# Moving the first batch of cross-attention into the last unit of self-attention, and turning the product of scores and exponentials

## The chip, the cores and the metric

The kernel runs on one core of a Trainium2 chip. The metric is the device time of one execution in microseconds. The core has TensorE (PE, matrix products into PSUM), VectorE (DVE), ScalarE (ACT), GpSimd (POOL) and SyncE (SP, which here only issues DMAs). Each engine runs its own list of instructions in order; they wait for each other through semaphores that the code sets by hand.

## The reference

One decoder layer over x of shape (8, 256, 512) in float32, three residual steps:

```
x = x + self_attention(layernorm(x))     # 16 heads of 128; slots M = 64, causal, rope
x = x + cross_attention(layernorm(x), ctx, mask)   # 16 heads of 16, 512 x 512 scores per head and batch
x = x + feed_forward(layernorm(x))       # weights through an NF4 round trip, silu gate
```

Self-attention, per head, with q and k turned by rope and es = exp(clip(s)), enz = 1 / cumsum(es):

```
A  = causal(q @ k.T) * scale             # t x j
ok = enz * (A @ es)                      # t x 64
qv = softmax(ok)
W2 = causal((qv * enz) @ es.T)           # t x j
o  = W2 @ v;  y = (rmsnorm(o) * silu(g)) @ Wo.T     # q, k, v, g, s are projections of layernorm(x)
```

Cross-attention projects q from layernorm(x), k and v from ctx, with a mask on both sides, and takes a softmax over 512 positions.

## The kernel before, in words

`decoder` calls `self_attention`, `cross_attention` and `feed_forward`, each a block of its own; between two blocks all engines meet, and POOL clears the semaphores of the old block.

**Self-attention** works in 32 units n: two halves of the tokens, eight groups g of two heads, two token blocks p of 512. Each engine has a function `unit(n, g, p, k0)` written by hand, which also holds the second stage of unit m = n - 1 and the third of unit l = n - 2, so that the engines' chains overlap. `units` calls it for the first three units and the last of each half, and in a hardware loop for those between; `core(LAST, 1)` then drains what is left of unit 31. Projections are done in split precision: a value's high part (fp32r) is made by ACT, its low part by POOL, and three products of four matrix steps replace one. On PE a unit is: `project_qk` 0, `project_s` (scores of ws2), `project_out` tiles 0 and 1 of unit l, `ok(m)`, `project_qk` 1, `project_out` 2 and 3, transposes of es, `project_qk` 2, transposes of qv, and so on to `out_transposes(m)` (the letters in `a_ogh`, `a_ogl` are the high and low parts of unit l's gated output, made by ACT and POOL out of these transposes).

`ok(m)` (L969 to L971) multiplies for each head and pair of token blocks: stationary a block of 128 x 128 of `a_aw` (masked scores), moving 64 columns of `a_es`. The result lies in PSUM (`pok`, the fourth bank of `a_mid`) with tokens on the partitions. DVE scales it by enz (`okn`, L676) and takes the maximum (L680), POOL subtracts it (L552), ACT takes exp (L447), POOL multiplies by enz (L558), PE transposes it (L996). DVE's units of the loops carry 31 instructions each of the NF4 round trip of the feed-forward weights besides, in fixed places (`nf4`).

In four units (`PREPS`) the next 512 tokens are normalised, transposed and split into `xh` and `xl`; the tile `xs` holds the raw tokens.

**Cross-attention** starts with the rows of the mask (`mask_products`, L1478 to L1493, 8 partitions x 512), stored to DRAM (`rows_scratch`). For each batch: layernorm, six products (`project(b, j)`: j = 0, 1 for q, 2, 3 for k, 4, 5 for v, plain float32), split of q and k into `hi` (ACT) and `lo` (POOL), stored to DRAM (`parts_scratch`, `put_part`) and loaded again as stacks `Q[b % 3]` and `K[b % 3]`, in which 48 rows of a head's three-part product and 5 or 6 rows of the mask stand below each other (`fill_stack`, `mask_rows`). Then 32 quarters t (four heads each): `row_scores` on PE and `row_max` on DVE find each row's maximum two quarters ahead (LEAD = 2), `turn_max` transposes them, DVE negates them (`max_rows`), SP stores and loads them as the last row of Q (`rows`), and only then `dot` and the exponential may run. All loads and stores but a few stand in one list on SP, in the order in which the code issues them.

The head of cross-attention before is: project(0, 0 to 5), wait for stack 0, scores of unit 0, `turn_max(0)`, project(1, 0 to 5), scores of unit 1, dots.

## Time and profile before

| | us |
|---|---|
| median of 3 runs | 2444.95 |
| lowest, highest | 2437.4, 2446.93 |
| the profiled execution | 2442.58 |
| its span | 2440.8 |
| PE busy | 2211.7 (91%) |
| DVE busy | 1612.8 (66%) |
| ACT, POOL busy | 776.0 (32%), 756.5 (31%) |

Self-attention fills the time up to about 1468 us, cross-attention runs from 1478 to about 2120, feed-forward to the end. Busy times are sums over stages with different limits, so a row of the whole span only says where to look; the stretch in question is read from the instructions in order of time. There each row has its start, its duration, the engine, the line of the kernel, output and inputs, the shapes and a count; the bracket at the end is the idle time of the engine in front of the row and what ended it. Products overlap by their ends, so the distance between two starts says more than a duration.

### The profile page before, as it was taken

Reading aid. Unit: us, or ns where it says so; the run is one execution under the profiler, and the core shown is the slowest. Engines: PE = TensorE matmul, PEld = TensorE weight load, DVE = VectorE, ACT = ScalarE, POOL = GpSimd, SP = SyncE. Lnnn points to the kernel's source line nnn. Section 1 sums busy time; section 2 is a strip of 40 time slices with the busy share of each in tenths; the row PEclk is TensorE's granted clock in tenths of the full one; section 3 lists DMA queues with packets and bytes.
Section 4 is the critical chain, followed back from the end, with each engine's and each line's share of the span. In section 5 each row is a group of like instructions: output and inputs, shape, how many; then the busy total and the mean of one; then the engine's idle time right before and its main releaser. Section 6 shows DMA issues by size and latency. Waiting matters only on the chain. (4 is left out here: it accounts for less than half of the span.)

```text
span 2440.8 us, 35529 instructions
## 1 busy us (share of the span) xinstructions
PE 2211.7 (91%) x11766; PEld 1577.0 (65%) x11766; DVE 1612.8 (66%) x2879; ACT 776.0 (32%) x1804; POOL 756.5 (31%) x531
## 2 busy tenths in 40 slices
PE   6899999999999999999999973788988897679998
PEld 4778888888877888888888861333333332257777
DVE  6668788888866568878887733567777777442221
ACT  1213323222332332232223120154454555532221
POOL 3324433433442443453353322111112221111222
PEclk9899999999999999999999986688788998869999
DMA  5211101101111201110110006825565554301100
GB/s 186 84 38 50 49 13 55 50 15 47 49 50 62 70 15 42 49 55 6 55 49 18 3 18 150 137 82 102 117 127 124 120 107 90 101 35 52 52 35 18
DMA packets 58085, 157.21 MB, mean 64 GB/s; under 512 B 9510, under 2 KB 24302, under 8 KB 51446
## 3 DMA queue, kind: packets, MB, share of 16 engines
q1 hardware_dynamic: 56742, 153.55, 23.7%
q10 hardware_dynamic: 1248, 2.46, 0.6%
q8 instruction: 52, 0.85, 0.2%
q14 instruction: 43, 0.35, 0.1%
HBM read 113.25 MB, written 34.33 MB: 60 GB/s over the span
## 5 line engine op out<-in xcount | busy, mean ns | idle before, releaser
L1501 DVE TENSOR_REDUCE x_mx<-x_pm 128x1 f32<-128x512 f32 x512 | 316.1, 679 | 76.5 <-PE x_pm L1598 75.3
L1334 ACT ACTIVATE x_E<-x_pd 128x512 f32<-128x512 f32 x512 | 265.5, 603 | 226.6 <-PE x_pd L1612 225.6
L1598 PE MATMUL x_pm<-x_K,x_Q 53*128 53x512 f32 x512 | 191.2, 514 | 44.7 <-DMA x_K<-parts_scratch 24.7
L659 DVE TENSOR_TENSOR a_rm<-a_pj,a_rope 128x1024 f32<-128x1024 f32 x128 | 155.8, 1218 | 113.0 <-PE a_pj L930 111.4
L1612 PE MATMUL x_pd<-x_Q,x_K 54*128 54x512 f32 x512 | 180.5, 514 | 49.8 <-DMA x_Q<-maxima_scratch 25.0
L1612 PEld LDWEIGHTS x_pd<-x_Q,x_K 54*128 54x128 f32 x512 | 76.9, 203 | 225.3 <-ACT x_E L1334 116.2
L442 ACT ACTIVATE a_v<-a_pj 128x256 f32<-128x256 f32 x128 | 49.1, 384 | 414.6 <-PE a_pj L946 414.6
L568 POOL TENSOR_TENSOR a_ogl<-a_ogf,a_ogh 128x512 fp32r<-128x512 f32 x64 | 81.3, 1291 | 292.7 <-ACT a_ogf L473 292.7
L1626 PE MATMUL x_pa<-x_E,x_vx 128*32 128x512 f32 x1024 | 153.4, 675 | 0.0
L930 PE MATMUL a_pj<-a_xh,a_wqk_h 128*128 128x512 f32 x512 | 150.8, 416 | 1.3 <-POOL a_wqk_l L538 1.3
L946 PE MATMUL a_pj<-a_wvg_h,a_xh 128*128 128x512 f32 x512 | 151.0, 417 | 1.0 <-DVE a_rm L659 1.0
L930 PE MATMUL a_pj<-a_xh,a_wqk_l 128*128 128x512 f32 x512 | 140.9, 397 | 0.0
L946 PE MATMUL a_pj<-a_wvg_l,a_xh 128*128 128x512 f32 x512 | 140.5, 396 | 0.0
L930 PE MATMUL a_pj<-a_xl,a_wqk_h 128*128 128x512 f32 x512 | 140.3, 396 | 0.0
L946 PE MATMUL a_pj<-a_wvg_h,a_xl 128*128 128x512 f32 x512 | 140.1, 395 | 0.0
L1598 PEld LDWEIGHTS x_pm<-x_K,x_Q 53*128 53x128 f32 x512 | 81.8, 210 | 89.4 <-DVE x_mx L1501 56.1
L720 DVE TENSOR_TENSOR a_acc<-a_po,a_acc 128x512 f32<-128x512 f32 x128 | 88.2, 689 | 66.2 <-PE a_po L1049 66.0
L1732 POOL TENSOR_TENSOR f_hl<-f_hf,f_hh 128x512 fp32r<-128x512 f32 x44 | 56.6, 1285 | 212.2 <-ACT f_hh L1773 212.2
L1049 PE MATMUL a_po<-a_wo_h,a_ogh 128*128 128x512 f32 x256 | 106.5, 416 | 16.2 <-POOL a_ogl L568 16.2
L665 DVE RECIPROCAL a_enz<-a_mid 128x512 f32<-128x512 f32 x32 | 107.2, 3351 | 7.8 <-PE a_mid L914 7.8
L1373 POOL TENSOR_TENSOR x_lo<-x_lo,x_hi 128x512 fp32r<-128x512 f32 x32 | 40.7, 1271 | 231.1 <-ACT x_hi L1329 231.1
L930 PEld LDWEIGHTS a_pj<-a_xl,a_wqk_h 128*128 128x128 f32 x512 | 96.5, 189 | 23.7
(209 smaller groups left out, 4919.4 us busy)
## 6 DMA issues: line engine op xcount, KB each, us to landing
a_qk_raw<-in_wqk SPq DMA_DIRECT2D x16, 1024.0 KB, 5.4
a_vg_raw<-in_wvg SPq DMA_DIRECT2D x16, 1024.0 KB, 4.9
x_Q<-parts_scratch SPq DMA_DIRECT2D x42, 256.0 KB
x_K<-parts_scratch SPq DMA_DIRECT2D x42, 256.0 KB
a_wo_raw<-in_wo SPq DMA_DIRECT2D x16, 512.0 KB, 3.6
parts_scratch<-x_hi SPq DMA_DIRECT2D x16, 512.0 KB, 2.8
parts_scratch<-x_lo SPq DMA_DIRECT2D x16, 512.0 KB, 3.3
a_acc<-in_w SPq DMA_DIRECT2D x6, 704.0 KB, 4.5
```

What stands on the lines that cost most here:

```text
L568: nc.gpsimd.tensor_tensor(ogl[:, h, :], ogf[:, h, :], ogh[:, h, :].bitcast(F32), ALU.subtract).then_inc(ogl_done, 1)
L659: nc.vector.tensor_tensor(turned, pb, table, ALU.mult).then_inc(roped_m, 1)
L665: nc.vector.reciprocal(enz[:, p], ps[:, 0, :].rearrange("p (t m) -> p t m", t=4)).then_inc(enz_done, 1)
L720: nc.vector.tensor_tensor(a, po[:, tt % 2, :], a, ALU.add).then_inc(added, 1)
L930: last = mm(pj[:, j % 2, :], wa[:, c, j * P:(j + 1) * P], xa[:, c, p * UT:(p + 1) * UT], start=k == 0, stop=k == 11)
L946: last = mm(pj[:, tt % 2, :], xa[:, c, t0:t0 + P], wa[:, c, :], start=k == 0, stop=k == 11)
L1049: last = mm(po[:, tt % 2, :], oa[:, h, tt * P:(tt + 1) * P], wa[:, h, :], start=k == 0, stop=k == 5)
L1334: nc.scalar.activation(E[:, n % ESLOTS, :], pd[:, n % 3, :], ACT.Exp, scale=XD ** -0.5).then_inc(exp_done, 1)
L1501: nc.vector.reduce_max(mx[:, u % 2, at:at + 1], pm[:, k % 3, :], AX_X).then_inc(pm_done, 1)
L1598: mm(pm[:, k % 3, :], Q[b % 3][z, hp, q * P:(q + 1) * P], K[b % 3][z, hp, :], start=True, stop=True).then_inc(pm_ready, 1)
L1612: mm(pd[:, n % 3, :], K[b % 3][z, hp, q * P:(q + 1) * P], Q[b % 3][z, hp, :], start=True, stop=True).then_inc(dot_ready, 1)
L1626: last = mm(pa[32 * i:32 * i + 32, 0, :], vx[:, b % 3, q, head(t, i)].rearrange("p d k -> p (d k)"), E[:, k % ESLOTS, :], start=q == 0, st ...
```

## The change

1. `ok(m)` is turned: stationary 64 columns of `a_es`, moving the 256 or 128 columns of `a_aw`. Head 0 writes PSUM partitions 0 to 63, head 1 partitions 64 to 127. The result has the slots on the partitions, so ACT copies it to a new tile `okT` (`turned_ok`) and PE transposes it back (`transposes_ok`) into the same bank. It stands in front of the output products of unit l, the transposes behind them.
2. Except in the units of `PREPS`, `project_s` on PE and `clip` on DVE are first in their unit.
3. The mask rows are made at the start of the kernel by DVE, in lines of tiles that are not yet in use, and stored to DRAM in eleven stores; no row is computed in cross-attention.
4. In the last unit DVE and POOL normalise the first batch of cross-attention (`variances(4)`, `normalised(4)`), which SP has loaded into `xs` with the first batch of ctx. In `core` PE does its four products of q and k (`project_cross`), DVE evacuates them (`take_cross`), ACT and POOL split them, SP stores the parts and fills stack 0.
5. `xh` and `xl` of self-attention and the stacks Q0 and K0 are views of one tile `q_big` that lives over all three parts (in feed-forward it holds w3 and xh). SP waits at the end of self-attention until the stack is filled.
6. Cross-attention starts with the scores of unit 0; then come the two products of v of batch 0, `turn_max(0)`, project(1, 0 to 5), scores of unit 1. Stack 1 is filled in six steps during the first six quarter steps, behind the maxima. Statistics and normalisation of later batches are split over two steps each.

What is the order in a unit of self-attention on PE? Before (L1036 transposes of the gated output, L930 the first product of q, L903 the scores, L1049 the output products of which 12 stand here, L969 ff. ok):

```order
L1036 MATMUL a_po<-a_ident,a_gs 128x128 x8
L930 MATMUL a_pj<-a_xh,a_wqk_h 128x512 x4
L930 MATMUL a_pj<-a_xh,a_wqk_l 128x512 x4
L930 MATMUL a_pj<-a_xl,a_wqk_h 128x512 x4
L903 MATMUL a_mid<-a_ws2x,a_s1x 128x128 x4
L1049 MATMUL a_po<-a_wo_h,a_ogh 128x512
...
L969 MATMUL a_mid<-a_es,a_aw 128x64
L970 MATMUL a_mid<-a_es,a_aw 128x64
```

After, the same place (L1057 was L903, L1084 was L930, L1138 is ok, L1213 was L1049, L1145 the transposes of okT):

```order
L1200 MATMUL a_po<-a_ident,a_gs 128x128 x8
L1057 MATMUL a_mid<-a_ws2x,a_s1x 128x128 x4
L1084 MATMUL a_pj<-q_big,a_wqk_h 128x512 x4
L1084 MATMUL a_pj<-q_big,a_wqk_l 128x512 x4
...
L1138 MATMUL a_mid<-a_aw,a_es 64x256 x2
L1138 MATMUL a_mid<-a_aw,a_es 64x128 x2
...
L1213 MATMUL a_po<-a_wo_h,a_ogh 128x512
...
L1145 MATMUL a_mid<-a_ident,a_okT 128x128 x4
```

The scores moved in front of the first product, ok in front of the output products, and its transposes behind them.

The head of cross-attention on PE, before (L1580 products of q and k, L1585 of v, L1598 scores for the maxima, L1603 the turn of the maxima, L1612 dots):

```order
L1580 MATMUL x_pp<-x_xn,x_wq 128x512 x2
L1580 MATMUL x_pa<-x_xn,x_wq 128x512 x2
L1580 MATMUL x_pp<-x_cx,x_wk 128x512 x2
L1580 MATMUL x_pa<-x_cx,x_wk 128x512 x2
L1585 MATMUL x_pp<-x_wv,x_cx 128x256 x4
L1585 MATMUL x_pa<-x_wv,x_cx 128x256 x4
L1598 MATMUL x_pm<-x_K,x_Q 128x512 x16
L1603 MATMUL x_pm<-x_ident,x_mx 128x128
```

After (L1720 scores, L1709 products of v, L1725 the turn, L1704 products of q and k, L1734 dots):

```order
L1720 MATMUL x_pm<-q_big 128x512 x16
L1709 MATMUL x_pp<-x_wv,x_cx 128x256 x4
L1709 MATMUL x_pa<-x_wv,x_cx 128x256 x4
L1725 MATMUL x_pm<-x_ident,x_mx 128x128
L1704 MATMUL x_pp<-x_xn,x_wq 128x512 x2
...
L1720 MATMUL x_pm<-q_big 128x512 x16
L1734 MATMUL x_pd<-q_big 128x512 x2
```

The first batch's products of q and k are gone from here, and the scores stand in front of everything.

SP's list at the end of self-attention, after (before, only the stores to x_scratch stood here behind those to weights_scratch):

```order
L463 DMA parts_scratch<-a_wqk_h 128x1024
L463 DMA parts_scratch<-a_wqk_l 128x1024
L126 DMA q_big<-rows_scratch 5x8x512 x2
L126 DMA q_big<-rows_scratch 6x8x512 x2
L133 DMA q_big<-parts_scratch 16x4096 x6
L368 DMA x_scratch<-a_acc 128x512 x4
L463 DMA parts_scratch<-a_wqk_h 128x1024
L463 DMA parts_scratch<-a_wqk_l 128x1024
L133 DMA q_big<-parts_scratch 16x4096 x6
L368 DMA x_scratch<-a_acc 128x512 x4
```

Q's parts and stack stand in front of the first four stores of x1, K's between these and the last four.

The core of the diff, functions of one engine together:

```diff
 # self_attention, SP
+            sp.wait_ge(rows_b, 6)
+            for i, line in enumerate(mq + mk):
+                sp.dma_start(rows_dram[:, i, :], line).then_inc(rows_out, 16)
...
+            def put(w, out):
+                n = slice(2 * w, 2 * w + 2)
+                for part, (tile, done) in enumerate(((xhi, chi_done), (xlo, clo_done))):
+                    sp.wait_ge(done, 2 * w + 2)
+                    sp.dma_start(split_dram[part, w], tile[:, n].bitcast(F32)).then_inc(out, 16)
+
+            put(0, cq_out)
+            sp.wait_ge(vg_ready, 4 * ALL_UNITS)
...
+            sp.wait_ge(cq_out, 32)
+            for e in range(2):
+                for seg in range(3):
+                    fill_part(sp.dma_start, Q0, 0, e, seg, split_dram, stack_0)
             store(1, 0)
+            put(1, ck_out)
+            sp.wait_ge(ck_out, 32)
...
             store(1, 1)
+            sp.wait_ge(stack_0, 16 * 16)
 # ACT
+            def turned_ok(m):
+                act.wait_ge(okT_ready, 8 * m + 8)
+                after(act, ok_ready, m)
+                nc.scalar.activation(okT[:], pok[:, 0, :], ACT.Copy).then_inc(okT_done, 1)
...
             def core(m, pm):
                 high_out(m - 1)
+                turned_ok(m)
+                cross_high(0)
+                cross_high(1)
                 exponent(m)
+                cross_high(2)
                 turned_es(m)
+                cross_high(3)
                 turned_qv(m)
 # POOL
             def core(m, pm):
                 low_out(m - 1)
+                cross_low(0)
+                cross_low(1)
                 below_max(m)
                 scaled(m, pm)
+                cross_low(2)
+                cross_low(3)
 # DVE
             def core(m, pm):
+                take_cross(0)
+                take_cross(1)
                 add_out(m - 1, 1 - pm, (0, 1))
                 ok_chain(m, pm)
+                take_cross(2)
                 add_out(m - 1, 1 - pm, (2, 3))
                 ok_sum(m)
                 ok_eps(m)
+                take_cross(3)
...
+            mask_products()
             variances(0)
 # PE
             def ok(m, pm):
...
-                for i in range(4):
-                    b, h = i // 2, i % 2
-                    pe.wait_ge(a_masked, 4 * m + i + 1)
-                    last = causal(lambda t: pok[:, 0, (2 * b + t) * P + h * M:(2 * b + t) * P + (h + 1) * M],
-                                  aw[:, i, :], lambda t: es[:, pm, t, h * M:(h + 1) * M], b)
+                for b in range(2):
+                    for lhs, cols, out in ((2 * b, slice(0, 2 * P), 0), (2 * b + 1, slice(2 * P, 3 * P), P)):
+                        for h in range(2):
+                            i = 2 * b + h
+                            pe.wait_ge(a_masked, 4 * m + i + 1)
+                            width = cols.stop - cols.start
+                            last = mm(pok[h * M:(h + 1) * M, 0, 2 * b * P + out:2 * b * P + out + width],
+                                      es[:, pm, lhs, h * M:(h + 1) * M], aw[:, i, cols], start=out == 0, stop=out > 0)
+                            last.then_inc(okT_ready, 1)
...
             def core(m, pm):
+                project_cross(0)
+                project_cross(1)
+                ok(m, pm)
                 project_out(m - 1, ALL_GROUPS - 1, (0, 1))
-                ok(m, pm)
+                transposes_ok(m)
+                project_cross(2)
                 project_out(m - 1, ALL_GROUPS - 1, (2, 3))
+                project_cross(3)
                 transposes_es(m, pm)
 # cross_attention, SP
+        SECOND = [(0, (0, 1)), (0, (2, 3)), (0, (4, 5)), (1, (0, 1)), (1, (2, 3)), (1, (4, 5))] + 10 * [(0, ())]
...
-                    if b and b + 1 < B:
-                        stack(b + 1, *FILLS[G])
+                    if b + 1 < B:
+                        stack(b + 1, *(FILLS if b else SECOND)[G])
 # DVE
-            mask_products()
+            dve.wait_ge(filled, 2)
+            for q in range(4):
+                row_max(0, q)
+            max_rows(0)
             dve.wait_ge(const_in, N_CONST)
...
+            take_projection(0, 4)
+            for ct in range(2):
+                norm_stats(1, ct)
+            take_projection(0, 5)
+            for ct in range(2):
+                norm(1, ct)
```

## Rows read from the trace of the kernel before

**Rows 1.** Busy time by stretch, PE PEld DVE ACT POOL, granted clock, DMA share, GB/s
```profile
400.00:600.00 200.00, 198.31 (x1181) 162.11 (x1180) 164.57 (x310) 56.68 (x165) 76.42 (x47) 1.00 0.11 36
...
1580.00:1585.00 5.00, 0.00 (x0) 0.00 (x0) 0.00 (x0) 0.00 (x0) 0.00 (x0) 0.50 1.04 128
```

**Rows 2.** TensorE in order of time, one unit of self-attention: start, us, instructions
```profile
1087.35 0.33 PE L969 MATMUL a_mid<-a_es,a_aw 128*128 128x64 f32 x2
...
1089.95 1.17 PE L930 MATMUL a_pj<-a_xh,a_wqk_h 128*128 128x512 f32 x4
...
1095.61 0.60 PE L990 MATMUL a_mid<-a_ident,a_es 128*128 128x128 f32 x4
1095.96 1.18 PE L930 MATMUL a_pj<-a_xh,a_wqk_h 128*128 128x512 f32 x4
...
1098.85 0.60 PE L996 MATMUL a_mid<-a_ident,a_okn 128*128 128x128 f32 x4
```

**Rows 3.** TensorE in order of time: row products, column products
```profile
710.28 1.58 PE L962 MATMUL a_mid<-a_qr,a_kr 64*128 64x256 f32 x16
711.78 1.20 PE L946 MATMUL a_pj<-a_wvg_h,a_xh 128*128 128x512 f32 x4
...
1649.75 1.07 PE L1626 MATMUL x_pa<-x_E,x_vx 128*32 128x512 f32 x8
```

**Rows 4.** The page's costliest groups: busy and mean ns, idle before
```profile
L1049 PE MATMUL a_po<-a_wo_h,a_ogh 128*128 128x512 f32 x256 | 106.5, 416 | 16.2 <-POOL a_ogl L568 16.2
```

**Rows 5.** ACT, DVE and POOL in order of time, same unit as rows 2
```profile
1085.68 0.63 ACT L482 ACTIVATE a_es<-a_es 128x512 f32<-128x512 f32 x1 [1.13 <-DVE a_es L646]
...
1090.76 0.68 DVE L676 TENSOR_TENSOR a_okn<-a_mid,a_enz 128x512 f32<-128x512 f32 x1
...
1094.30 1.29 POOL L558 TENSOR_TENSOR a_okn<-a_prob,a_enz 128x512 f32<-128x512 f32 x1 [0.75 <-ACT a_prob L447]
```

**Rows 6.** Start of the kernel, and the mask instructions in cross-attention
```profile
5.07 0.69 DVE L615 BATCH_NORM_STATS2 a_stats<-a_xs 128x6 f32<-128x512 f32 x1 [5.07 <-DMA a_xs<-in_x]
...
9.79 1.94 PE L879 MATMUL a_pj<-a_ident,a_xs 128*128 128x128 f32 x8 [9.79 <-DVE a_xs L625]
...
1479.59 0.41 DVE L1478 TENSOR_SCALAR x_lo<-x_lo 8x512 f32<-8x512 f32 x1 [10.13 <-DMA x_lo<-in_mask]
...
1484.43 0.41 DVE L1493 TENSOR_SCALAR x_K<-x_lo 8x512 fp32r<-8x512 f32 x1
```

**Rows 7.** TensorE in order of time, from self-attention to cross-attention
```profile
1428.07 0.47 PE L1049 MATMUL a_po<-a_wo_h,a_ogh 128*128 128x512 f32 x1 [3.50 <-POOL a_ogl L568]
...
1460.13 0.77 PE L1049 MATMUL a_po<-a_wo_h,a_ogh 128*128 128x512 f32 x1 [2.97 <-POOL a_ogl L568]
...
1468.33 0.40 PE L1049 MATMUL a_po<-a_wo_h,a_ogl 128*128 128x512 f32 x1
...
1492.63 3.75 PE L1580 MATMUL x_pp<-x_xn,x_wq 128*128 128x512 f32 x4 [23.90 <-DVE x_xn L1455]
...
1498.27 1.88 PE L1580 MATMUL x_pp<-x_cx,x_wk 128*128 128x512 f32 x4
...
1522.21 1.22 PE L1598 MATMUL x_pm<-x_K,x_Q 53*128 53x512 f32 x3 [16.89 <-DMA x_K<-parts_scratch]
...
1533.09 3.62 PE L1580 MATMUL x_pp<-x_xn,x_wq 128*128 128x512 f32 x4
...
1545.89 0.73 PE L1598 MATMUL x_pm<-x_K,x_Q 53*128 53x512 f32 x3
...
1560.21 0.80 PE L1612 MATMUL x_pd<-x_Q,x_K 54*128 54x512 f32 x2 [4.35 <-DMA x_Q<-maxima_scratch]
...
1590.15 0.80 PE L1612 MATMUL x_pd<-x_Q,x_K 54*128 54x512 f32 x2 [13.01 <-DMA x_Q<-maxima_scratch]
```

**Rows 8.** SP's queue in order of time, head of cross-attention
```profile
1478.04 0.30 SPq L1204 DMA_DIRECT2D x_lo<-in_mask  x1
...
1558.93 2.61 SPq L1186 DMA_DIRECT2D x_Q<-parts_scratch  x6
```

394 lines of the change are left out of this document (221 added, 173 removed).

## The prediction

> **What bounds the kernel now.** I read the busy time by stretch first. In the steady part of self-attention TensorE is busy 198.31 of 200 us at the full granted clock [rows 1]: whatever is taken from TensorE's own work there comes off the time, and whatever another engine does costs nothing until TensorE waits for it. Then I read TensorE's own order of time over the passage from self-attention to cross-attention [rows 7], because the shares of the whole span hide it. The reader should see a row of waits: TensorE ends self-attention at 1468.7, starts the first projections of cross-attention at 1492.63 (23.9 us idle), waits 16.89 us for the stacks, does 16 score products (1522.21), then the second batch's projections (1533.09 to 1545.89, 12.8 us) and 16 more scores, and starts the first dots at 1560.21. The dots of the second quarter start only at 1590.15, after a wait of 13.01 us for the negated row maxima. That wait is a queue: twelve fills of stack 1 (256 KB each, first six issued from 1558.93 [rows 8]) keep the DMA engines full at 128 GB/s as late as 1585 [rows 1], and the maxima stand behind them. So the change aims at two places: TensorE's work in 31 units, and the 122 us from 1468.3 to 1590.15.
>
> **Part 1, the turned first product (once in each of 31 units).** Before, ok is 12 products with a stationary a_aw block of 128 columns and 64 moving columns. They take from 1087.35 to 1089.95, 2.60 us [rows 2]. After, it is 8 products, 4 of 256 and 4 of 128 moving columns, whose stationary is a 64-column block of a_es, heads alternating between the lower and the upper 64 PSUM partitions. Each product is two instructions. The trace has no product of this shape. Bounds: the row products L962 have just these widths (4 of 256, 4 of 128), alternate between two halves of the rows, and take from 710.28 to 711.78, 1.50 us [rows 3]. One after the other these 1536 columns would take 2.56 us (1024 plain columns take 1.88 us with their end, 1.7 without it, in the row at 1498.27 [rows 7]). The rows nearest in kind are the column products L1626, four groups of 32 columns, 512 moving columns each: 8 instructions in 1.07 us [rows 3], against 3.41 us one after the other by the same count. So groups of columns do overlap here, and I take 1.50 us plus 0.09 for the change of form (the gap in front of such a group). Then come four transposes of okT, as the four of a_es: 1095.61 to 1095.96, 0.35 us [rows 2]. Net per unit: 2.60 - 1.59 - 0.35 = 0.66 us less; if the columns did not overlap, 2.60 - 2.65 - 0.35 = 0.40 us more.
>
> The Trainium skill (TensorE: Matmul & The Clock Gate, "Measured speedup vs the span model") gives 2.38x for three column groups of 32. An estimate from it, at the same share of the ideal, is 1.59x for two groups, so 1.61 us in place of 1.50; the sum would gain 3.4 us less over 31 units. The row L1626 (3.2x with four groups) does a little better than that page. Another page speaks against the form: by the Trainium skill (TensorEngine Tiling (Array Packing), "Key Properties") changing the tiling mode drains the engine. No row here separates that price from the 0.1 us gaps that are already in the sum.
>
> Between ok and its transposes there is now an evacuation on ACT. Its cover on TensorE is the pair of output products, 12 x 0.23 = 2.8 us, against one ACT copy of 512 columns, 0.6 us as that of a_es [rows 5]. In units that load a new group ACT has the high parts and the exponential in front, and ended them at 1085.68 + 0.63 = 1086.3 [rows 5]. The new ok starts 3.6 us before the old one (which had the output products, 2.8 us, the wait of 0.35 and L903 in front), so at 1083.7; it ends at 1085.3, ACT copies until 1086.9, and TensorE comes to the transposes at 1088.1. Cost nothing, with 1.2 us of cover left.
>
> Order in the unit: the output products now stand behind ok, 1.6 us later. Before, TensorE waited there for POOL's a_ogl: 16.2 us in all [rows 4], of which 3.50 and 2.97 lie in the last stretch (1428.07 and 1460.13 [rows 7]). The 9.7 us that are left, some 0.35 a unit, go away. The scores' product of ws2 (L903) moves next to the transposes in front of it, and clip next to it on DVE: equal work, at zero.
>
> What is late next: the chain okn, max, subtract, exp, times enz. It ends at 1094.30 + 1.29 = 1095.6 [rows 5], and its transposes start at 1098.85 [rows 2], 3.3 us of cover. TensorE will come there 1.0 us earlier in the unit, and DVE's own chain starts up to 1.3 us later (the output adds stand in front of it and now wait for later products). Some 1 us of cover is left, but in the units where DVE works without a pause it will hold back a part of the gain. I take off 4 us of 30. **Sum of part 1:** 31 x 0.66 = 20.5, plus 9.7, less 4, is **26 us less**. Bounds: 31 us less; or, without overlap, 31 x 0.40 = 12 us more, less 9.7, 3 us more with nothing held back, 7 with it.
>
> **Part 2, the start.** The 13 mask instructions of 8x512 on DVE now stand in front of the first statistics. In cross-attention 12 of them took from 1479.59 to 1484.84, 5.3 us [rows 6], 1.55 us after their load was issued at 1478.04 [rows 8]. DVE starts at 5.07 when x lands, and TensorE's first transposes at 9.79 wait for DVE [rows 6]. If the mask is there at about 3 us, DVE is free at 8.3: **3.2 us more**. Bounds: 1.8 (the mask is there at 1.55, as after its load in cross-attention) to 5.3 (it lands with x). The eleven small stores to rows_scratch sit on SP ahead of the load of x(1), which waits for transposes anyway: zero.
>
> **Part 3, the last unit and the drain of self-attention.** Added on TensorE: four cross products (two of 512 plain columns each, four passes: 2 x 512 x 4 / 2.4 GHz = 1.7 us, which the row at 1498.27 gives as 1.88 with its end [rows 7]), 6.9 us, and 0.35 for the transposes. Two of the products stand where TensorE waited 3.50 us in front of the output product at 1428.07 [rows 7]; the other two and the transposes lengthen the stretch up to the transposes of qv, where the chain of part 1 left TensorE standing anyway. Behind them wait ACT (four high parts of 0.6), POOL (four low parts of 1.3) and DVE (four evacuations of 0.75). Only one of these stands directly in front of the chain: the last high part in front of the copy of qvT. I get 1 us more (-2 to +3).
>
> The stores and fills on SP. Q's first two cross products end at 1424.6 + 3.4 = 1428.0, ok 1.6 later; ACT copies okT and makes the two high parts by 1431.5, POOL the low parts by 1434; they land about 1437.5; six fills of 256 KB at 128 GB/s take 12.3 us; then 1 MB of x1 and 1 MB of K's parts (16 us at that rate; long rows go faster, so I take 10); then six fills of K, 12.3 us: about 1473. SP waits for this stack in front of the end of the block. Before, the last product ended at 1468.7, sum and store take some 3 us, and SP issued the first load of cross-attention at 1478.04 [rows 8]. So the wait on the stores is replaced by a wait on K's fills that ends some 2 us later. With 1 us for TensorE and 1 for some 13 more semaphores to clear: cross-attention starts **4 us later**, at 1482 (0 to 12).
>
> **Part 4, the head of cross-attention.** From its start S: scores of unit 0 at once, paced by DVE at 0.6 us each, to S + 9.8; the two value products at the lower clock level, 6.9 us (3.4 at the upper); the turn at S + 17; then DVE has to negate the maxima, take v, and do the statistics and the normalisation of batch 1, with POOL's root behind POOL's values: 5 us in which TensorE stands. The second batch's projections 12.8 and scores 10 as before: first dots at S + 44.5 = 1526.5, against 1560.21. Gone are the wait for the stacks and the first batch's four projections of q and k in front of it. The quarter itself took 29.9 us, 13.0 of them the wait for the maxima. Now only two fills stand in front of those, 4 us of DMA time under a quarter of 17 us, so they are on time: second quarter at 1543.5. The fills of stack 1 are spread over six steps up to its first use 36 us on, and take 25 us of full DMA; I add 2 us for a wait there. 1590.15 - 1545.5 = **44.6 us less**. Later batches keep their order; the split statistics I take at zero (3 us to either side). Feed-forward gets other addresses for the same work: zero.
>
> **Sum.** -26 + 3.2 - 44.6 = -67.4 us. The profiled execution took 2442.58 (span 2440.8), so 2375.2; the median of the runs is 2.4 higher: **2378 us**.
>
> **The rivals.**
> 1. No overlap of the column halves. For it: the trace has no 64-column group. Against it: L1626. Price 31 x 1.06 = 33: 2411 us.
> 2. The DMA engines become the bound of the passage: K's fills land 8 us later than I say (all fills and stores share 128 GB/s), and the maxima wait 4 us at the second quarter and 3 more at the third. Price 15: 2393 us. For it: 1.04 as DMA share in the old wait.
> 3. The passage keeps TensorE at the upper clock level, since it stands less: 3.4 us in the value products, 2.5 in the projections, 4 in the first quarter, 2 in the drain: 2366 us. Against it: the granted clock is 0.50 at 1580 to 1585, while TensorE stands [rows 1].
> 4. The change does not do what it says: the stack is not ready at the block's end and SP holds everybody until fills of 3 MB (25 us) are through, so only part 1 is left: about 2422 us.
> 5. Slower: in every unit the transposes of okT find ACT's copy late. It decides from 80 / 31 = 2.6 us of standing per unit beyond the 1.2 us of cover; at 3.5 us per unit it gives 2378 + 31 x 3.5 = 2486.5 us. For it: one more step in a chain over four engines. Against it: ACT's share and the cover above.
>
> **How the numbers follow.** Forecast 0.52, rival 1 0.12, rival 2 0.18, rival 3 0.10, rival 4 0.05, rival 5 0.03. The range 2356 to 2412 takes in the forecast with its bounds (start 2, drain 8, unit 5) and rivals 1 to 3; rivals 4 and 5 and half of the tail of 3 stay outside. Half a per cent, 12 us, is about what a measurement can tell from no change. Faster by more than that: 0.95; within it 0.02; slower 0.03.
>
> **What would show it.** In the profile after: ok's eight products 1.5 us and no wait for a_ogl in front of the output products; units shorter by 0.8 to 1.0 us; DVE's first statistics near 8.3 us; TensorE's scores at once when cross-attention starts, 9 to 13 us after the last output product; the first dots 44 us after that; a wait for maxima at the second quarter of under 4 us. A wait of TensorE in front of the okT transposes, or ok at 2.6 us, or SP waiting for fills long after the last sum would make it wrong.

## The result, and the profile after

| | before | after |
|---|---|---|
| median of 4 runs, us | 2445.94 | 2406.51 |
| lowest, highest | 2437.4, 2449.55 | 2392.86, 2415.64 |
| profiled execution, its span | 2442.58, 2440.8 | 2406.03, 2404.3 |

The ratio is 0.9837, with a 95% interval of 0.9804 to 0.9871: about 40 us less. The forecast was 67 us less. The direction and most mechanisms held, the size did not. Between marks of the two profiled executions the time moved as follows (the start of a mark is that of TensorE's first instruction after it; the start of cross-attention in the kernel before is SP's first load, because TensorE's first product there waits until 1492.63):

| stretch | before, us | after, us | moved | forecast |
|---|---|---|---|---|
| start of the kernel to first projection | 21.46 | 23.88 | +2.4 | +3.2 |
| to the end of unit 31's first stage (1424.57; 1418.21) | 1403.1 | 1394.3 | -8.8 | -26 |
| to the start of cross-attention (1478.04; 1479.63) | 53.5 | 61.4 | +7.9 | +4 |
| to the dots of the second quarter (1590.15; 1539.93) | 112.1 | 60.3 | -51.8 | -48.6 |
| to the last turn of the maxima (2093.51; 2052.54) | 503.4 | 512.6 | +9.2 | 0 |
| to feed-forward's first product (2132.49; 2095.78) | 39.0 | 43.2 | +4.3 | 0 |
| to the end | 308.3 | 308.5 | +0.2 | 0 |

**The steady units.** TensorE in order of time, in the changed kernel (start, duration, instructions): one even unit, in which L1138 is the turned product, L1213 the output products, L1145 the transposes of okT. The last row is from the odd unit behind it.

```profile
994.89 1.52 PE L1138 MATMUL a_mid<-a_aw,a_es 128*64 128x256 f32 x16
996.35 0.50 PE L1213 MATMUL a_po<-a_wo_h,a_ogh 128*128 128x512 f32 x1
...
999.26 0.60 PE L1145 MATMUL a_mid<-a_ident,a_okT 128*128 128x128 f32 x4
999.62 1.18 PE L1084 MATMUL a_pj<-q_big,a_wqk_h 128*128 128x512 f32 x4
...
1058.86 0.94 PE L1174 MATMUL a_mid<-a_qvT,a_esT 64*128 64x256 f32 x3 [0.59 <-DVE a_aw L841]
```

The turned product takes 1.46 us (994.89 to 996.35) where it took 2.60 [rows 2], its transposes 0.36, and there is no wait in front of them. The profile's row of the output products, with its idle time behind the bar, has 3.0 us of waits for a_ogl left of 16.2 [rows 4], all in one wait:

```profile
L1213 PE MATMUL a_po<-a_wo_h,a_ogh 128*128 128x512 f32 x256 | 106.1, 414 | 3.0 <-POOL a_ogl L666 3.0
```

So the pieces cost what the forecast said, and still a unit (from one `out_transposes` to the next) went from 42.97 us to 42.42 in even units and to 43.18 in odd ones, 42.80 in the mean. The new wait stands in the last row of the first fence: TensorE waits for DVE's evacuation of the second weights (L841, which masks them on their way out of PSUM). DVE in order of time, in that odd unit, and one row of POOL:

```profile
1040.47 0.69 DVE L862 TENSOR_TENSOR a_acc<-a_po,a_acc 128x512 f32<-128x512 f32 x1 [1.70 <-PE a_po L1213]
1041.88 0.69 DVE L862 TENSOR_TENSOR a_acc<-a_po,a_acc 128x512 f32<-128x512 f32 x1 [0.72 <-PE a_po L1213]
...
1050.78 1.61 DVE L171 TENSOR_TENSOR a_pos<-a_pos,a_lev 128x704 bf16<-128x704 bf16 x1
...
1058.26 1.01 DVE L841 TENSOR_TENSOR a_aw<-a_mid,a_mask 128x384 f32<-128x384 f32 x2
```
```profile
1050.36 1.65 POOL L630 TENSOR_TENSOR a_qr<-a_rm 128x512 f32<-128x512 f32 x1
```

DVE stands 1.70 us for the output products (0.49 before), which now come behind the turned product. From 1048.41 on it works without a pause and reaches L841 4.0 us after the product that it evacuates has started (1054.26); before, this was 2.2 us. Of these 1.8 us, 1.0 is TensorE, which comes sooner in the unit. The other 0.8 is not the stand by itself: at 1049.61 DVE is only 0.1 us later in the unit than before (16.68 us behind the transposes of the gated output, 16.57 before). Then L171 takes 1.61 us beside POOL's L630, where the same instruction took 0.51 in this unit of the kernel before, and takes 0.51 again in e5 below. So the stand pushed a DVE instruction beside one of POOL's, and that one was stretched.

**From self-attention to cross-attention.** TensorE, in order of time (the last output product; first scores, projections of batch 1 and dots of cross-attention; the dots of the second quarter), the rows that answer [rows 7]:

```profile
1458.64 0.39 PE L1213 MATMUL a_po<-a_wo_h,a_ogl 128*128 128x512 f32 x1
...
1479.63 1.19 PE L1720 MATMUL x_pm<-q_big 53*128 53x512 f32 x3 [20.59 <-PEq L107]
...
1500.07 3.63 PE L1704 MATMUL x_pp<-x_xn,x_wq 128*128 128x512 f32 x4 [5.10 <-DVE x_xn L1602]
...
1521.41 1.21 PE L1734 MATMUL x_pd<-q_big 54*128 54x512 f32 x2
...
1539.93 0.79 PE L1734 MATMUL x_pd<-q_big 54*128 54x512 f32 x2
```

The 16.89 and 13.01 us of [rows 7] are gone, and scores, 5.1 us of standing for the normalisation, and first dots 41.8 us after the start (forecast 44.5) are near what was foretold. But 20.59 us of idle time stand in front of the first scores, where 9 to 13 were expected. SP's queue in order of time, and what SP waited for from 1425 to 1482 (us in all, times, longest):

```profile
1435.94 0.45 SPq L463 DMA_DIRECT2D parts_scratch<-a_wqk_l  x1
1454.48 2.64 SPq L133 DMA_DIRECT2D q_big<-parts_scratch  x6
1457.16 2.95 SPq L368 DMA_DIRECT2D x_scratch<-a_acc  x4
1479.59 0.34 SPq L1385 DMA_DIRECT2D x_cx<-in_ctx  x1
```
```profile
SPq L133 <- DMA parts_scratch<-a_wqk_l: 19.6, 2, 18.1
SPq L483 <- DMA x_scratch<-a_acc: 11.5, 1, 11.5
```

K's parts are issued at 1435.9 and have landed only 18.1 us later, behind Q's six fills and the first 1 MB of x1. K's fills (1.5 MB) and the second 1 MB of x1 share the DMA engines from 1454.48 on. SP waits 11.5 us for the last of these stores, until 1471.6, and the next block begins at 1479.6, 20.9 us after TensorE's last product has started (9.7 before).

**The later batches.** SP and TensorE in the changed kernel, around a new wait. Up to 1613.91 SP issues fills of the next stack, at 1614.60 the store of the maxima, and it stands until that has landed (1623.98), with K's last three fills behind it:

```profile
1613.91 0.58 SPq L133 DMA_DIRECT2D x_K<-parts_scratch  x1
1614.60 0.35 SPq L1417 DMA_DIRECT2D maxima_scratch<-x_mT  x1
1623.98 0.52 SPq L1420 DMA_DIRECT2D x_Q<-maxima_scratch  x2
1624.55 1.23 SPq L133 DMA_DIRECT2D x_K<-parts_scratch  x3
...
1633.14 0.80 PE L1720 MATMUL x_pm<-x_K,x_Q 53*128 53x512 f32 x2 [5.18 <-DMA x_K<-parts_scratch]
```

What TensorE waited for from 1541 to 2053 in the changed kernel, then from 1591 to 2094 in the kernel before (us, times, longest):

```profile
PE x_pm L1720 <- DMA x_K<-parts_scratch: 23.9, 5, 6.3
...
PE x_pm L1720 <- DVE x_mx L1627: 8.3, 20, 1.0
PE x_pm L1720 <- DMA q_big<-parts_scratch: 7.9, 2, 4.5
```
```profile
PE x_pm L1598 <- DVE x_mx L1501: 15.5, 16, 3.7
PE x_pm L1598 <- DMA x_K<-parts_scratch: 7.8, 2, 6.1
```

7 us of waits for the row maxima went, and 24 us of waits for K's fills came (31.8 in all, with 7.9 us in two waits on the stack in `q_big`, against 7.8). In the quarter with the wait at 1633.14 the granted clock is 0.81, in the one ahead of it 1.00. Windows of the changed kernel (span, busy of PE, PEld, DVE, ACT, POOL, granted clock, DMA share, GB/s): the quarter before that wait, the quarter with it, and the end of cross-attention; then the end of cross-attention in the kernel before:

```profile
1608.60:1627.60 19.00, 17.66 (x79) 6.38 (x77) 15.23 (x25) 9.77 (x19) 2.54 (x2) 1.00 0.85 125
1627.60:1654.10 26.50, 20.06 (x87) 8.65 (x85) 13.26 (x22) 9.88 (x19) 7.11 (x8) 0.81 0.32 75
...
2053.00:2096.00 43.00, 23.20 (x105) 6.19 (x105) 8.34 (x11) 17.76 (x35) 5.20 (x5) 0.66 0.24 75
```
```profile
2094.00:2132.00 38.00, 17.85 (x102) 5.25 (x101) 8.30 (x11) 17.71 (x35) 5.19 (x5) 0.82 0.26 83
```

The quarter with the wait takes 26.5 us and the one ahead of it 19.0. In the kernel before, the same two took 22.7 (at 0.73, behind the wait for the row maxima) and 18.5 (at 1.00): 4.3 us less for the pair.
### The profile page after: what moved, and what is told of

It is laid out like the page before. It is cut to its first block and busy times, and to the rows that moved or that the text cites. A ratio compares the mean times of both kernels' runs of the same rounds, so it can differ in the third digit from the quotient of the medians.

```text
span 2404.3 us, 35495 instructions
## 1 busy us (share of the span) xinstructions
PE 2189.0 (91%) x11638; PEld 1535.4 (64%) x11638; DVE 1602.9 (67%) x2880; ACT 791.9 (33%) x1836; POOL 761.2 (32%) x532
## 5 line engine op out<-in xcount | busy, mean ns | idle before, releaser
L1084 PE MATMUL a_pj<-q_big,a_wqk_h 128*128 128x512 f32 x1024 | 290.0, 405 | 1.0 <-POOL a_wqk_l L634 1.0
L1100 PE MATMUL a_pj<-a_wvg_h,q_big 128*128 128x512 f32 x1024 | 286.1, 406 | 1.1 <-DVE a_rm L790 1.0
L1100 PEld LDWEIGHTS a_pj<-a_wvg_h,q_big 128*128 128x128 f32 x1024 | 185.3, 188 | 51.8 <-DVE a_rm L790 2.4
L1084 PEld LDWEIGHTS a_pj<-q_big,a_wqk_h 128*128 128x128 f32 x1024 | 182.9, 188 | 40.4 <-POOL a_wqk_l L634 1.5
L1720 PE MATMUL x_pm<-x_K,x_Q 53*128 53x512 f32 x320 | 112.6, 484 | 32.1 <-DMA x_K<-parts_scratch 23.9
L1100 PE MATMUL a_pj<-a_wvg_l,q_big 128*128 128x512 f32 x512 | 140.7, 397 | 0.0
L1084 PE MATMUL a_pj<-q_big,a_wqk_l 128*128 128x512 f32 x512 | 140.1, 395 | 0.0
L1734 PE MATMUL x_pd<-x_Q,x_K 54*128 54x512 f32 x320 | 109.3, 494 | 21.5 <-ACT x_E L1490 17.3
L1734 PEld LDWEIGHTS x_pd<-x_Q,x_K 54*128 54x128 f32 x320 | 45.5, 196 | 127.8 <-ACT x_E L1490 72.2
L1100 PEld LDWEIGHTS a_pj<-a_wvg_l,q_big 128*128 128x128 f32 x512 | 96.7, 189 | 23.5
L1084 PEld LDWEIGHTS a_pj<-q_big,a_wqk_l 128*128 128x128 f32 x512 | 96.0, 187 | 23.4
L1213 PE MATMUL a_po<-a_wo_h,a_ogh 128*128 128x512 f32 x256 | 106.1, 414 | 3.0 <-POOL a_ogl L666 3.0
```

The source lines that it names most:

```text
L1084: last = mm(pj[:, j % 2, :], wa[:, c, j * P:(j + 1) * P], xa[:, c, p * UT:(p + 1) * UT], start=k == 0, stop=k == 11)
L1100: last = mm(pj[:, tt % 2, :], xa[:, c, t0:t0 + P], wa[:, c, :], start=k == 0, stop=k == 11)
L1213: last = mm(po[:, tt % 2, :], oa[:, h, tt * P:(tt + 1) * P], wa[:, h, :], start=k == 0, stop=k == 5)
L1720: mm(pm[:, k % 3, :], Q[b % 3][z, hp, q * P:(q + 1) * P], K[b % 3][z, hp, :], start=True, stop=True).then_inc(pm_ready, 1)
L1734: mm(pd[:, n % 3, :], K[b % 3][z, hp, q * P:(q + 1) * P], Q[b % 3][z, hp, :], start=True, stop=True).then_inc(dot_ready, 1)
```

## The experiments

Two things are read in each: the median against the kernels beside it, and the marks of its profiled execution. The marks of self-attention repeat to within 0.1 us per unit from kernel to kernel. In the batches of cross-attention they do not, and there TensorE's idle time has to be read apart from its busy time, which the granted clock stretches. From the third turn of the maxima to the last:

| code of the batches | profiled kernels | the stretch, us | TensorE idle, us | granted clock |
|---|---|---|---|---|
| as before | before, e12 | 502.6, 499.9 | 54.6, 60.8 | 0.88, 0.90 |
| as changed | e1, after, e7, e4, e5, e2 | 508.0, 511.9, 512.3, 523.4, 524.3, 527.5 | 76.0, 74.0, 70.1, 75.3, 71.5, 68.8 | 0.92, 0.90, 0.90, 0.88, 0.88, 0.86 |
| e6 | e6 | 507.5 | 55.1 | 0.87 |
| e3 | e3 | 511.5 | 47.0 | 0.85 |
| e8 | e8, e9 | 488.4, 475.8 | 44.1, 46.5 | 0.89, 0.93 |
| e10 | e10 | 488.0 | 57.9 | 0.92 |
| e8 in the kernel before | e11 | 489.0 | 45.5 | 0.89 |

The same code takes 508 to 527 us: its idle time stays within 69 to 76 us, and the same instructions keep TensorE busy for 432 us at a clock of 0.92 and for 459 at 0.86. Each kernel has one profiled execution, and no run shows what decides the clock there. So up to 20 us of a difference in this stretch can be the clock alone, and an edit in it is judged by the idle time.

**e1: the turned product undone.** The old 12 products behind the output products, no okT:

```diff
-                if began(n, 1):
-                    ok(m, pm)
                 if began(n, 2):
                     project_out(l, g - 1, (0, 1))
                 if began(n, 1):
-                    transposes_ok(m)
+                    ok(m, pm)
```

> The changed kernel with the old first product (12 products in front of nothing, no okT, output products ahead of it); all else as changed. Theory A (the turned product is nearly used up, because DVE now reaches the evacuation of the second weights late in every unit): 5 to 9 us slower than the changed kernel's 2406, so 2411 to 2415, and all units between 42.9 and 43.1 us. Rival B (the turned product is worth the predicted 26 us and the missing gain lies elsewhere): 2430 to 2434. The wait for a_ogl comes back with about 16 us in either case.

Measured: 2407.15 us (2405.37 to 2420.25). All units 42.97 us again; the last output transposes of self-attention start at 1459.82 instead of 1446.26, 13.6 us later, and cross-attention 8.5 us later (1488.16): SP's wait for the last stores of x1 in between is 7.2 us instead of 11.5. The last turn is 8.1 us later. The medians stand 0.6 apart, with ranges of 15 and 23 us, outside both theories, and decide nothing. By the marks the turned product is worth 13.6 us at the end of self-attention, more than theory A's 5 to 9, and 8.5 at the start of cross-attention; B's 26 is at neither. The wait for a_ogl came back, with 7.5 us in all (16.2 in the kernel before, 3.0 in the changed one), less than both theories said.

**e12: the turned product alone, in the kernel before**, with its order of scores and clipping (the same edit of `ok`, `turned_ok`, `transposes_ok`, `clip`, and `sq` in bf16 as in the changed kernel; nothing of cross-attention).

> The kernel before with the turned first product alone, with its order of the scores' product and of the clipping. Theory A (the loss is DVE's in every odd unit, not a matter of the shared tile): units of 42.42 and 43.18 again, the last unit 6 to 8 us earlier than before, 2438 to 2442. Rival B (the new order in units comes from the shared tile or the rest of the change): all units near 42.0, 2420.

Measured: 2427.18 us (2421.01 to 2442.88) against 2444.7, ratio 0.9926 (0.9899 to 0.9953). Units of 42.42 and 43.18 us: theory A's mechanism. The gain is larger than A's 3 to 9 us and less than B's: 17.5 us. The marks show 7.7 us up to unit 30, of which 2.7 lie ahead of the first output transposes, and 12.5 at the last ones, because unit 31's tail shrinks from 31.66 to 26.93 us: the wait of 3.50 us for a_ogl [rows 7] is 2.06, and TensorE is busy 3.6 us less, at a granted clock of 0.87 instead of 0.80. So the turned product is worth 12.5 us there in the one kernel and 13.6 in the other (e1). The first projection starts at 21.47 as in the kernel before, and the output transposes of the first unit that has them at 111.57. In the changed kernel they start at 114.15, and at 113.34 to 114.56 in e3 to e6 and e8, which have the same start. So the start's term, 2 to 3 us, is real and is kept.

**e2: DVE's first nf4 group ahead of the adds**, into the hole of 1.70 us:

```diff
+                nf4(n, p, k0, 0)
                 if began(n, 2):
                     add_out(l, p, (0, 1))
-                nf4(n, p, k0, 0)
```

> The changed kernel with DVE's first nf4 group of a unit (4 or 5 instructions, 1.9 to 2.2 us) ahead of the output adds, where DVE stands 1.7 us for the later output products. Theory A (the second weights' evacuation is late because DVE stands in that hole and then works without a pause): TensorE's wait for a_aw goes, units fall from 42.42 and 43.18 to about 42.1 and 42.2, 18 us over the units with nf4 work, 2388 to 2394. Rival B (the lateness is ACT's or POOL's chain): units as they are, 2403 to 2409. Rival C (the adds then come late and hold the output products' banks): units over 43, 2410 or more.

Measured: 2400.05 us (2395.98 to 2410.74), between the ranges of A and B. Odd units fell from 43.18 to 41.97, even ones rose from 42.42 to 43.33. DVE and POOL in order of time, in an even unit of e2:

```profile
990.91 4.38 DVE L158 TENSOR_TENSOR a_wt<-a_wt,a_inv 128x704 bf16<-128x704 bf16 x1
```
```profile
989.94 4.60 POOL L638 TENSOR_TENSOR a_wvg_l<-a_vg_raw,a_wvg_h 128x2048 fp32r<-128x2048 f32 x1 [0.20 <-ACT a_wvg_h L502]
```

The group's first instruction, 0.88 us elsewhere, took 4.38: it ended 0.8 us after POOL's subtraction of 4.60 us (989.94 to 994.54). Only even units have that subtraction there. So the odd units' loss hangs on DVE's order, and the place that heals it in one unit is blocked in the other.

**e5: the same in odd units alone** (`if p == 1:` ahead, `if p == 0:` behind the adds).

> The changed kernel with DVE's first nf4 group ahead of the output adds in the odd units alone (there the units fell from 43.18 to 41.97 us; in the even ones POOL's subtractions stretch the group's first instruction from 0.88 to 4.38 us and the units rose from 42.42 to 43.33). Theory A (DVE's order is all that holds the gain back): odd units 41.97, even ones 42.42, the end of self-attention 12 to 15 us earlier than in the changed kernel (its last output transposes at 1431 to 1434 instead of 1446.3), 2391 to 2395 in all. Rival B (odd and even units share one loss, which only moves from one to the other): even units rise to 43 or more, 2400 or more.

Measured: 2394.28 us (2383.43 to 2403.03), units 41.97 and 42.42, the last output transposes at 1432.17, 14.1 us earlier than in the changed kernel. Theory A holds by the marks; the median is in its range, with a spread of 20 us. 41.97 is the 42.97 of before less the 1.0 us that the forecast took for a unit that nobody holds back. In these units L171 takes 0.51 us again and not 1.61: how much of the cure is the earlier order and how much the lost meeting with POOL, the run does not tell apart.

**e3: K's fills ahead of the wait for the stored maxima** in cross-attention's steps, and the last of K's one step earlier.

```diff
-        FILLS = [(0, (2,)), (0, (3,)), (0, (4, 5)), (1, (0, 1)), (1, (2,)), (1, (3,)), (1, (4, 5))] + 9 * [(0, ())]
+        FILLS = [(0, (2,)), (0, (3,)), (0, (4, 5)), (1, (0, 1)), (1, (2, 3)), (1, (4, 5))] + 10 * [(0, ())]
...
+                    if b and b + 1 < B:
+                        stack(b + 1, *FILLS[G])
                     if q == 1 and t + 1 < QUADS:
                         rows(t + 1)
...
```

> The changed kernel with the fills of the next stack issued ahead of the wait for the stored maxima in cross-attention's steps, the last of K's one step earlier. Theory A (the second quarter of each batch is long, 26.5 us, because SP stands on the store of the maxima for 9.4 us with K's last three fills behind it): the scores' waits for K's fills fall from 31.8 us to under 10, the steps that took 26.5 us take 21 to 22, 2385 to 2395. Rival B (DMA is full and the fills land at the same time whoever issues them): the waits move to the maxima rows in front of the dots, 2400 to 2410.

Measured: 2393.59 us (2389.94 to 2400.03). What TensorE waited for in the later batches of e3:

```profile
PE x_pd L1736 <- DMA x_Q<-maxima_scratch: 10.1, 6, 2.4
PE x_pd L1736 <- DMA q_big<-maxima_scratch: 7.9, 5, 3.0
...
PE x_pm L1722 <- DMA x_K<-parts_scratch: 1.9, 1, 1.9
```

The wait for K's fills fell from 31.8 us to 1.9, so it was SP's order. But 18.0 us of waits for the maxima stand in its place (8.7 in the changed kernel), in shorter pieces. TensorE's idle time in the batches fell from 74.0 to 47.0 us, so B's shift is only a part. The median is where A put it, but the profiled execution gained only 0.4 us from the third turn of the maxima to the last (511.5 us against 511.9): it ran there at 0.85 instead of 0.90, and TensorE was busy 26.6 us longer with the same instructions. The granted clock took the gain of this execution away.

**e6: statistics and normalisation in one piece**, at their old places (steps 2 and 4 of a batch).

> The changed kernel with the statistics and the normalisation of the later batches of cross-attention each in one piece at its old place. Theory A (splitting them took away a wait of 3 to 4 us for the row maxima and gave back one of 5 to 6 us for K's fills, a trade): the wait for the row maxima of 3 us is back, those for K's fills fall under 12 us in all, the last turn of the maxima 2 to 9 us earlier or equal against the changed kernel, 2398 to 2406. Rival B (the place of the statistics has nothing to do with the long quarters, the fills are late in the new order anyway): waits for K's fills stay over 20 us, and the wait for the row maxima comes on top, 2410 to 2420.

Measured: 2400.25 us (2394.45 to 2411.39), within the spread of the changed kernel. Waits for the row maxima 12.7 us (8.3), for K's fills 11.6 (31.8); the last turn 4.2 us earlier. TensorE's idle time in the batches is 55.1 us, as in the kernels with the old code (54.6 and 60.8) and not as in the six with the changed one (69 to 76). Theory A, and more: the split was no even trade, it cost some 14 to 21 us of idle time, which the medians do not show clearly.

**e8: the maxima on another queue.** Store and return are issued by ACT, after the exponentials of the first and the second step of a quarter; SP keeps fills, loads and stores.

```diff
-                    if q == 1 and t + 1 < QUADS:
-                        rows(t + 1)
...
 # ACT
...
+                    if q == 0 and t + 1 < QUADS:
+                        maxima_out(t + 1)
+                    if q == 1 and t + 1 < QUADS:
+                        maxima_back(t + 1)
```

> The changed kernel with the store of the maxima and their way back into the stack issued from ACT's queue instead of SP's, for all units but the first. Theory A (the maxima stand in SP's queue behind the fills, and SP stands behind the maxima with K's last fills): both waits go, the waits for K's fills and for the maxima fall under 8 us in all instead of 40, the clock falls less often, quarters take 19, 18.5, 13 and 13.5, and the last turn is 25 to 50 us earlier, 2356 to 2381. Rival B (the DMA engines are shared, so the maxima wait for the same bytes whatever queue they are in): waits move or stay, 2400 to 2410. Rival C (ACT stands for the maxima and holds the exponentials up): quarters of 12.7 become 14 or more, over 2410.

Measured: 2378.21 us (2363.67 to 2380.59), ratio to before 0.9702 (0.965 to 0.9754). The longest stand of ACT as TensorE saw it, in the first quarter of e8, and then TensorE's waits from 1546 to 2035:

```profile
1537.82 0.79 PE L1748 MATMUL x_pd<-q_big 54*128 54x512 f32 x1 [6.18 <-ACT x_E L1488]
```
```profile
PE x_pd L1748 <- ACT x_E L1488: 31.1, 75, 3.7
...
PE x_pd L1748 <- DMA x_Q<-maxima_scratch: 3.5, 2, 2.4
PE x_pd L1748 <- DMA q_big<-maxima_scratch: 2.4, 1, 2.4
```

There is no wait for K's fills any more and 5.9 us for the maxima; ACT gives 8.7 us of that back (31.1 against 22.4), where it stands for a stored maximum. The batches take 488.4 us from the third turn to the last, with 44.1 us of idle time, instead of 508 to 527 with 69 to 76; the first quarter lost 6 us to ACT's stand. The profiled executions are 25.5 us apart: 18.0 at the last turn, 4.7 at the end of cross-attention, where the clock did not fall early, and 2.8 in feed-forward, whose code is the same. Theory A, with C's mechanism in small. The 8 KB store of the maxima landed 1.3 us after its issue (median) in ACT's queue, and 4.1 us after it in SP's, with the fills. The Trainium skill (DMA: Bandwidth & Descriptors, "Queues, rings and completion order") says that each DMA engine takes turns between the queues for which it has work; the trace agrees, with these two landing times.

**e11: the same edit in the kernel before.**

> The kernel before with the maxima on ACT's queue, as in e8. Theory A (the queue's order was a bound before the change too, so the later batches' loss after it is an old bound in a new place): the waits for K's fills and maxima of batches 2 on (15.5 us) go, and the 13 us in front of the second quarter shrink to under 6: 2415 to 2430 against 2447. Rival B (only the changed kernel's order has the clash): 2440 to 2449.

Measured: 2431.24 us (2424.51 to 2442.01), ratio 0.9934 (0.9905 to 0.9963): 13.5 us, A's mechanism, a little outside its 2415 to 2430. The 13.01 us wait became 6.0 plus a stand of ACT of 6.5. The queue's order was a bound before the change too, and the same edit is worth about twice as much behind it (28 us by the medians).

**e4: K's parts stored ahead of x1.**

```diff
-            store(1, 0)
             put(1, ck_out)
+            store(1, 0)
```

> The changed kernel with K's split parts stored to memory ahead of the first half of x1 at the end of self-attention. Theory A (cross-attention starts late because K's parts land 18.1 us after their issue, behind 1.5 MB of fills and 1 MB of x1): they land 4 to 6 us earlier, the hole in the DMA traffic near 1450 goes, cross-attention starts 4 to 5 us earlier than 61.4 us after the last unit, 2401 to 2402. Rival B (the total of bytes sets the end, not their order): the end of the block stays within 1 us, 2405 to 2407.

Measured: 2405.32 us (2397.46 to 2406.08). K's fills were issued at 1452.95, 34.4 us after the last unit instead of 36.3, and cross-attention started 59.4 us after it instead of 61.4. K's parts landed 16.4 us after their issue instead of 18.1, so A's 4 to 6 us did not come, and half of its 4 us at the start of cross-attention did. The median lies in B's range and can't tell 2 us from none.

**e7: the mask behind the first low parts.** DVE's 13 instructions stand where DVE waited 4.8 us, their stores behind the next load of x.

> The changed kernel with the mask's 13 instructions behind the low parts of the first x on DVE (where DVE stands 4.8 us) and their eleven stores behind the load of the next x. By the prediction's start term TensorE's first projection comes 2.4 us earlier (21.5 instead of 23.9), and the output transposes of the second unit as well, at 111.8. Rival: the first units are bound by something else and give the start back, as they stand at 114.2 in both kernels: then still 114.2.

Measured: one execution, 2414.59 us. The first projection starts at 21.48, as foretold, and the first output transposes at 119.69: 5.5 us later, not 2.4 earlier. DVE and POOL in order of time, in e7:

```profile
16.93 4.77 DVE L725 TENSOR_SCALAR a_esT<-a_gs 8x512 fp32r<-8x512 f32 x1
21.63 4.79 DVE L727 CAST a_gs<-a_gs 8x512 fp32r<-8x512 f32 x1
```
```profile
16.82 4.60 POOL L634 TENSOR_TENSOR a_wqk_l<-a_qk_raw,a_wqk_h 128x2048 fp32r<-128x2048 f32 x1 [5.41 <-ACT a_wqk_h L497]
21.38 4.75 POOL L638 TENSOR_TENSOR a_wvg_l<-a_vg_raw,a_wvg_h 128x2048 fp32r<-128x2048 f32 x1
```

Two instructions of 0.41 us on 8 partitions took 4.8 each, as long as POOL's two subtractions, and TensorE waited 6.18 us for the scores' table behind them. Both of my theories missed that. The place in front of everything, where the change has the mask, has no such POOL work beside it, and there each takes 0.41 to 0.68 us.

**e9: three edits together** (e5, e8, e4).

> The changed kernel with three edits together: the nf4 group ahead of the adds in odd units (e5), the maxima on ACT's queue (e8), K's parts stored ahead of x1 (e4). If the three places are independent the gains add: 14.1 at the last unit, 2 at the start of cross-attention, 18 to 28 in its batches, so 2356 to 2372 with 2364 in the middle. Rival (cross-attention's phase decides by itself where the clock falls, and eats part of it): 2372 to 2382.

Measured: 2354.86 us (2348.51 to 2364.34), ratio to before 0.9637 (0.9593 to 0.968). The first marks add up: the last output transposes at 1431.72 (14.5 us earlier than in the changed kernel), cross-attention 60.1 us after the last unit. The batches took 475.8 us, 12.6 less than in e8 with the same code and about the same idle time (46.5 and 44.1), at a clock of 0.93 instead of 0.89: that part is the clock. The median is 1 us under A's range. It beats both kernels by far more than their spread: 90 us under before, 52 under after.

**e10: and two more.** The maxima's return one ACT step later in the first quarter of a batch, and two nf4 instructions of even units moved behind the evacuation of the second weights (places 4, 5, 4, 5, 7, 6 instead of 4, 6, 5, 4, 6, 6).

> As e9, and the maxima's way back is issued one ACT step later in the quarters after a batch's first, where ACT stood 2.5 to 6.2 us for the stored maxima; and in even units two of the eleven nf4 instructions ahead of the second weights' evacuation move behind it. Theory A (these two waits are what is left): even units 42.0 to 42.1 instead of 42.42, 5 us earlier at the last unit, ACT's stands gone and some clock falls with them, 5 to 15 us under e9. Rival (the later return makes the next quarter's dots wait for the maxima instead): ACT's stands are exchanged for waits of the dots, within 3 us of e9 less the 5.

Measured: 2375.92 us (2368.58 to 2386.57), 21 us over e9. Even units are 42.00 us now, so the second edit did what it should. The first did harm: the last turn is 10.6 us later than in e9, with 57.9 us of idle time in the batches instead of 46.5, and the clock fell early at the end of cross-attention (7.4 us more). TensorE's waits from 1530 to 2018 in e10:

```profile
PE x_pd L1751 <- DMA x_Q<-maxima_scratch: 18.4, 4, 6.1
PE x_pd L1751 <- DMA q_big<-maxima_scratch: 14.9, 3, 7.4
```

33.3 us of waits for the maxima against 6.2 in e9, where ACT's stands were 9 us longer: the rival, and worse than it said. ACT standing for a short time was the cheaper side.

## Why the forecast was right in direction and too large

**Right.** The price of the turned product (1.46 and 0.36 us against 1.50 and 0.35): the columns overlap, rival 1 fell. The end of all but one of the waits for a_ogl. ACT's copy in time, rival 5 fell. A unit at 41.97 us where nobody holds it back (e5). The start, 2.4 us of 3.2. The head of cross-attention, 60.3 us of 63.5, with its 5 us of standing and no wait for the maxima at the second quarter. The clock in the head, so rival 3 fell: 0.50 in the scores and in the first quarter, 0.64 in the value products, which took 5.5 us of 6.9.

**Wrong by the prediction's own signs.** It had units shorter by 0.8 to 1.0 us, and they moved by -0.55 and +0.21. It had TensorE's scores 9 to 13 us after the last output product, and they came 20.9 us after it, with SP waiting for its last transfers.

**Part 1, the step that was mis-sized: "What is late next".** It named the right effect, DVE's adds later by the turned product, but followed only one chain of DVE, ok to its exponential, found 1 us of cover and took off 4 us of 30. The instruction that had no cover was another one, 18 us further on in DVE's order: the evacuation of the second weights. It gave 0.45 us back in even and 1.2 in odd units, some 20 us in all. e2, e5 and e10 show that it was this and little more: in e10, where units take 41.97 and 42.00 us, the stretch from the first projection to the end of unit 31's first stage takes 1375.9 us, 27.2 less than before, against 30 in the forecast ahead of its 4 us. What made DVE late in the odd units was for the most part an instruction stretched beside POOL's; that two engines can hold each other up is in no term of the sum.

**Part 3, the drain: 7.9 us for 4.** Up to K's parts the sum held: it had them landed 35.2 us after the last unit, and they were there after 36.3. Behind them it gave "six fills of K, 12.3 us" and left out that the second 1 MB of x1 goes beside them. Together they took 17.1 us (1454.5 to 1471.6), 4.8 more, and that is the miss; 1.0 came back behind it (8.0 us to the next block, for 9). Rival 2 named the place, with fills 8 us late where they were 5 us late; its other half, the waits for the maxima at the second and third quarter, did not come. e4 moves 2 us of it by order alone.

**Part 4, "Later batches keep their order; the split statistics I take at zero".** This was 9.2 us wrong in the profiled executions, and is the second failure. What the sum had at zero was 19.4 us of idle time in TensorE (54.6 before, 74.0 after); the granted clock, 0.90 after 0.88, gave 10.2 us of it back, and that was luck: in the other five kernels with this code the error would be 5 to 25 us. The term is the split: with the statistics in one piece the idle time is 55.1 us (e6). They did save their wait, and the waits for the next stack's fills came for it; SP stood for a stored maximum with K's last three fills behind it. The text had seen the same queue in the kernel before [rows 1, 8], and did not ask what the six other batches would do when DVE let go. That SP's order carries the waits is shown by e3 (47.0 us of idle time) and e8 (44.1); how the split leads to them is read from SP's list, and no run separates it.

**The end of cross-attention, 4.3 us,** came from the clock alone in the profiled execution. Whether it falls there changes from one profiled execution to the next (e1 to e6, e8, e9 and e12 took 39 us for this stretch, e7, e10 and e11 43 to 46), and no run shows what sets it.

Together: 17.2 us in part 1 (26 less 8.8), 3.9 in the drain, 9.2 and 4.3 in cross-attention and 0.2 behind it make 34.8 that were missing; 0.8 at the start and 3.2 in the head came on top. That leaves 30.8, the difference between -67.4 and the measured -36.6.

The measured 2406.5 lies in the range of 2356 to 2412, near its upper end. The range was drawn for the bounds and rivals 1 to 3. Rivals 1 and 3 did not happen and rival 2 happened in part; that the range holds is in part luck, because the 20 us of part 1 and the idle time of the batches were in none of them.

## What to carry to other kernels

When a product is moved or made cheaper, follow every instruction that stands behind its consumers on the other engine, up to the next one that the first engine waits for, and not only the chain that the product itself feeds. When a wait is taken away in front of a list of transfers, ask what the list does when it is asked faster: here a transfer of a few KB stood in one queue with megabytes, and a queue of its own was worth 28 us by the medians, more than the turned product (17.5 in e12). DVE's idle time is only a free place if no long POOL instruction lies beside it. And read idle time and granted clock apart, before a gain or a loss of some us is given to an edit.

## What the runs showed of the hardware

- A DVE instruction can take more than ten times as long beside POOL: 0.41 became 4.77 and 4.79 us beside subtractions of 4.60 and 4.75 (e7), 0.88 became 4.38 beside one of 4.60 (e2), 0.51 became 1.61 beside one of 1.65 (changed kernel). In these rows it doesn't depend on its own size, 8 partitions or 128; it ends 0.3 to 0.8 us after POOL's ends. The Trainium skill (SBUF — State Buffer, "Who interferes with whom") says that two engines share a pair of ports which one of them holds for a whole instruction; the traces agree in these rows, for TENSOR_SCALAR, CAST and a TENSOR_TENSOR with both inputs in SBUF.
- Two groups of 64 columns overlap for the most part in float32: 1536 moving columns in 1.46 us, against an estimate of 2.56 one after the other, worked out in the forecast from [rows 7].
- The quarter that waited 5.18 us took 26.5 us at a granted clock of 0.81, against 18.5 at 1.00 in the kernel before. Over the batches the clock doesn't follow the waits so simply: the six kernels with the same code have 69 to 76 us of idle time and a clock of 0.86 to 0.92, e3 has 47 us and 0.85. No run here sets the clock by itself.
- A small transfer in a queue of its own passes what lies in the other one: the 8 KB store of the maxima landed after 1.3 us in ACT's queue (e8), after 4.1 (changed kernel) and 4.5 us (e3) in SP's with the fills. The waits for maxima were 5.9 us in e8 and 18.0 in e3.
